# Feed-forward product by tile pairs in seven block products in place of eight, and the output part stepping by pairs on more PSUM banks

## What is computed

```
h = x + LN( Attn( LN(x) ) )          # Wq, Wk, Wv, Wo: 1024x1024, 16 heads of 64, rotary, causal softmax
y = h + LN( FFN( LN(h) ) )           # LN without scale or shift, eps 1e-5
FFN(z) = z @ weight.T + bias + (z @ A.T) @ B.T     # weight 1024x1024; A, B: LoRA factors of rank 16
```

## Time and profile before

| | |
|---|---|
| median of 3 runs | 2083.32 us (2083.1 to 2083.62) |
| profiled execution: its time, its span | 2083.8 us, 2082.0 us |
| PE busy | 1981.3 us (95%), 12192 matmuls |
| DVE, ACT, POOL busy | 1425.8, 866.2, 393.2 us |
| chain of waits that ended last | PE 89%, DVE 4%, DMA 1% |
| costliest line | L603 (the products of the output part): 3072 matmuls |
| granted TensorE clock, mean | 0.979 of full |

### The profile page before, as it was taken

The page is one execution under the profiler, slowest core; times in us unless marked ns, Lnnn a source line. Parts: engine busy times, 40 slices in busy tenths (PEclk is TensorE's granted clock), DMA queues, the critical chain, the costliest instruction groups (busy, mean ns, idle before and its releaser), DMA issues.

```text
span 2082.0 us, 34087 instructions
## 1 busy us (share of the span) xinstructions
PE 1981.3 (95%) x12192; PEld 966.1 (46%) x12192; DVE 1425.8 (68%) x3455; ACT 866.2 (42%) x1985; POOL 393.2 (19%) x393
## 2 busy tenths in 40 slices
PE   4789999999999999999999997699999999999997
PEld 2344444444444444444444443354444444444443
DVE  5787787787787787687787778664554555555554
ACT  6655565565465565465565565421111111111111
POOL 0122222222222222222222222100000000000000
PEclk8999999999999999999999999799999999999998
DMA  8065376465375465375465575924334233433322
GB/s 309 5 128 112 78 143 109 83 142 102 76 145 106 84 141 102 75 144 108 83 141 102 121 205 127 270 74 122 92 76 113 77 102 74 119 102 72 81 61 61
DMA packets 492004, 232.40 MB, mean 112 GB/s; under 512 B 462801, under 2 KB 462929, under 8 KB 490802
## 3 DMA queue, kind: packets, MB, share of 16 engines
q1 hardware_dynamic: 491826, 230.10, 48.1%
HBM read 81.16 MB, written 33.55 MB: 55 GB/s over the span
## 4 chain that ended last, share of the span: by engine, by line
PE 89%; DVE 4%; issue 2%; POOL 1%; ACT 1%; DMA 1%; POOLq 0%; DVEq 0%; ACTq 0%; SPq 0%
PE ps L603 30%; PE ps L486 10%; PE ps L488 10%; PE ps L487 10%; PE ps L511 6%; PE ps L525 5%; PE ps L497 5%; PE ps L499 5%; PE ps L498 5%; PE ps L628 1%; DMA arena<-arena 1%; PE ps L638 1%; PE ps L637 1%; DVE region L692 1%; POOL turn L1182 0%
## 5 line engine op out<-in xcount | busy, mean ns | idle before, releaser
L486 PE MATMUL ps<-arena,region 128*128 128x512 f16 x1024 | 391.1, 382 | 11.0 <-DVE region L692 10.9
L487 PE MATMUL ps<-arena,region 128*128 128x512 f16 x1024 | 390.1, 381 | 0.0
L488 PE MATMUL ps<-arena,region 128*128 128x512 f16 x1024 | 390.1, 381 | 0.0
L877 DVE CUSTOM_DVE_ANT_0 ps<-ps,con,pow 128x384 f32<-128x384 f32 (+3 forms) x512 | 247.0, 555 | 146.9 <-PE ps L511 146.7
L603 PE MATMUL ps<-region,arena 128*128 128x512 f16 x1536 | 338.3, 380 | 0.0
L603 PE MATMUL ps<-region 128*128 128x512 f16 x1536 | 336.9, 379 | 0.2 <-issue 0.2
L1180 POOL TENSOR_TENSOR turn<-turn,con 128x512 f32<-128x512 f32 x128 | 144.3, 1127 | 894.4 <-DVE turn L734 877.2
L1102 ACT ACTIVATE ps<-ps,neg_max 128x384 f32<-128x384 f32 (+3 forms) x512 | 258.2, 510 | 91.9 <-DVE neg_max L877 91.9
L1141 ACT ACTIVATE arena<-ps,sm 128x1024 f32<-128x1024 f32 x64 | 77.1, 1205 | 472.9 <-DVE sm L952 472.9
L747 DVE SCALAR_TENSOR_TENSOR arena<-ps,row_inv,arena 128x384 f16<-128x384 f32 (+3 forms) x512 | 239.6, 542 | 1.0 <-ACT arena L1043 1.0
L1043 ACT ACTIVATE arena<-ps,row_inv 128x384 f16<-128x384 f32 (+3 forms) x512 | 221.2, 543 | 45.4 <-DVE row_inv L760 45.4
(11 more groups left out here) (120 smaller groups left out, 2235.6 us busy)
## 6 DMA issues: line engine op xcount, KB each, us to landing
arena<-x SPq DMA_DIRECT2D x32, 512.0 KB, 3.8
attn_scratch<-o_st SPq DMA_DIRECT2D x64, 256.0 KB, 2.4
region<-attn_scratch SPq DMA_DIRECT2D x8, 2048.0 KB, 8.7
turn<-x SPq DMA_DIRECT2D x32, 512.0 KB, 4.2
out<-v_split SPq DMA_DIRECT2D x32, 512.0 KB, 5.1
arena<-wo SPq DMA_DIRECT2D x8, 1024.0 KB, 7.0
arena<-wf SPq DMA_DIRECT2D x8, 1024.0 KB, 8.2
arena<-wv SPq DMA_DIRECT2D x4, 1024.0 KB, 11.8
```

Source lines behind the costliest of these rows:

```text
L486: mm(o, w[:, k, 0, cols], xnt[par][:, k, 0, :], start=(k == 0), stop=False)
L487: mm(o, w[:, k, 0, cols], xnt[par][:, k, 1, :], start=False, stop=False)
L488: last = mm(o, w[:, k, 1, cols], xnt[par][:, k, 0, :], start=False, stop=(k == KT - 1))
L877: v.tensor_tensor_reduce(out=unit_ps(j, a), in0=unit_ps(j, a), in1=causal[:, 512 - width:512], scale=pow2[:, S_NEG:S_NEG + 1], scalar=HIGH ...
```

## The change

The output part steps by pairs of tiles (`over_pairs`, 16 pairs, 18 steps). The feed-forward product of a pair is a 2x2 block product: the rows are tile 0 and tile 1, the inner dimension and the columns are in two halves of 512. Seven block products (each 4 k-blocks x 3 = 12 matmuls) take the place of eight, with sums of blocks as factors.

- **Weight**: seven fp16 pairs (W11, W22, T1, W21, T3, T2, T4) are made from W_F by `wf_prepare` on DVE (7 low parts and 4 sums for each half of the k-blocks, each 128x1024) and `wf_high_parts` on ACT. Half of this is at the end of the last attention slot, half in step 0.
- **Left side**: besides the four blocks of `xn2`, three sums S2, S4 and S3/S1 are made by four POOL operations (`mix`, 128x512). ACT and DVE split seven blocks where there were four, in operations of 1024, 1536, 512 and 512 columns. SP transposes 28 blocks in one DMA for the high parts, 8 and 20 for the low parts.
- **Products**: `block_product` into banks 4, 5 and 6, with copies of partial results to `y_out` by ACT (m5, m1, m6) and adds by DVE (c12, c22, c11).
- **Wo product**: tile 0 of a pair in banks 0 and 1, tile 1 in banks 2 and 3, both before the feed-forward product of the pair before.
- **`x` tiles**: four buffers. Those of pairs 0 and 1 are loaded in step 0. From step 2 on, SP issues the two loads for pair j in step j, behind the transposes and the stores.
- `lora_split` and `clear_lora` also make the differences `a_diff` and `b_diff`. W_F is loaded in another order.

```diff
@@ sync
+            def step(j, kind, bq, loads):
+                if 1 <= kind <= TP:
+                    need(sp, ff_done, j - 1)
+                    need(sp, x2_high, 4 * j)
+                    sp.nop(nofuse=True)
+                    sp.dma_start_transpose(xt[0][:, :, :], xh).then_inc(xt_h_in, 16)
+                    need(sp, x2_low_a, j)
+                    sp.nop(nofuse=True)
+                    sp.dma_start_transpose(xt[1][:, 0:8, :], xl_a).then_inc(xt_la_in, 16)
+                    need(sp, x2_low_s, 3 * j)
+                    sp.nop(nofuse=True)
+                    sp.dma_start_transpose(xt[1][:, 8:28, :], xl_s).then_inc(xt_ls_in, 16)
...
                 if kind >= 2:
+                    for t in range(2):
+                        slot_x = (2 * kind + t) % 4
+                        sp.wait_ge(y_done, 2 * j - 3 + t)
+                        sp.dma_start(out_tiles[2 * j - 4 + t], y_out[:, t]).then_inc(y_stored[t], 16)
+                        if kind < TP:
+                            sp.dma_start(x2[slot_x], x_tiles[2 * j + t]).then_inc(x_tile_in[slot_x], 16)
+                if kind % 2 == 1 and kind < TP - 4:
+                    sp.wait_ge(ao_done, 2 * j + 2)
+                    load_o(bq + 2, (kind // 2) % 2)
@@ tensor
+            def block_product(xb, wb, bank, start, ks=range(4)):
+                for k in ks:
+                    for hl, wl in ((0, 0), (0, 1), (1, 0)):
+                        last = mm(ps[:, bank, :], xt[hl][:, 4 * xb + k, :], wf[wb][:, k, wl, :],
...
             def step(j, kind, bq, loads):
+                if kind < TP:
...
+                    for a in range(2):
+                        need(pe, u1_done, 2 * j - 1 + a)
+                        if kind == 0 and a == 1:
+                            pe.wait_ge(p_done[1], 8 * PAIRS * B)
+                        ao_product(par, 2 * (kind % 2) + a, BANK_AO[a], kind == 0)
...
+                if 1 <= kind <= TP:
+                    need(pe, xt_h_in, 16 * j)
+                    need(pe, xt_la_in, 16 * j)
+                    need(pe, xt_ls_in, 16 * j)
+                    if kind == 1:
+                        pe.wait_ge(lora_ready, 2)
+                        pe.wait_ge(o_low, PAIRS * B)
+                        pe.wait_ge(wf_low, 14)
+                    need(pe, lt_scaled, j - 1)
+                    lora_first(0, ((A11, a_both, 0), (A12, a_both, 4)))
+                    lora_first(1, ((S1, a_both, 0), (A22, a_diff, 0))).then_inc(lt_done, 1)
+                    need(pe, c12_done, j - 1)
+                    block_product(S1, T1, BANK_53, True).then_inc(m5_done, 1)
+                    need(pe, u2_done[1], 2 * j - 2)
+                    block_product(A11, W11, BANK_U, True).then_inc(m1_done, 1)
+                    need(pe, m5_copied, j)
+                    block_product(S4, W22, BANK_53, False)
+                    need(pe, m1_copied, j)
+                    block_product(S2, T2, BANK_U, False).then_inc(m6_done, 1)
+                    need(pe, lt_low, j)
+                    lora_product(0, BANK_53, b_split[:, :, HALF:D]).then_inc(c12_ready, 1)
+                    need(pe, c11_done, j - 1)
+                    block_product(A12, W21, BANK_2, True, range(2))
+                    need(pe, m6_copied, j)
+                    block_product(S3, T3, BANK_U, False)
+                    lora_product(1, BANK_U, b_split[:, :, HALF:D]).then_inc(c22_ready, 1)
+                    block_product(A12, W21, BANK_2, False, range(2, 4))
+                    lora_product(0, BANK_2, b_split[:, :, 0:HALF]).then_inc(c11_ready, 1)
+                    need(pe, c22_done, j)
+                    block_product(A22, T4, BANK_U, False)
+                    lora_product(1, BANK_U, b_diff).then_inc(ff_done, 1)
@@ vector: order of one step
+            def step(j, kind, bq, loads):
+                if kind >= 2:
+                    need(dve, ff_done, j - 1)
+                    stats([c21, c22], st2[1], mv2[1], bn2_done, mv2_done, 2 * j - 3)
...
+                    s_low(j, 0, xl_s[:, 0:1536], xn2_f[:, 1024:2560], xh[:, 1024:2560])
...
+                    s_low(j, 1, xl_s[:, 1536:2048], xs2_f, xh[:, 2560:3072])
+                    s_low(j, 2, xl_s[:, 2048:2560], xs4_f, xh[:, 3072:3584])
...
+                        v.tensor_tensor(y_out[:, a], x2[(2 * kind + a) % 4], y_out[:, a], ALU.add).then_inc(y_done, 1)
+                if kind < TP:
+                    for a in range(2):
+                        residual(j, kind, bq, a)       # the residual chain; waits for x_tile_in before the add
+                if kind == 0:
+                    o_evac(PAIRS * B - 1, 1)
+                    wf_prepare(1, 0)
...
+                    v.tensor_scalar(t_part, ps[LOW_ROW:LOW_ROW + LR, BANK_T, 0:256], adapter[:, tile],
...
+                    v.tensor_tensor(t_stack[LOW_ROW:LOW_ROW + LR, :], t_f, t_stack[0:LR, :],
                                     ALU.subtract).then_inc(lt_low, 1)
+                if kind < TP:
+                    need(dve, x2_high, 4 * j + 1)
+                    need(dve, xt_la_in, 16 * j)
+                    v.tensor_tensor(xl_a, xn2[0], xh[:, 0:1024], ALU.subtract).then_inc(x2_low_a, 1)
+                if 1 <= kind <= TP:
...
+                    v.tensor_tensor(c12, ps[:, BANK_53, :], c12, ALU.add).then_inc(c12_done, 1)
...
+                    v.tensor_tensor(c22, ps[:, BANK_U, :], c22, ALU.add).then_inc(c22_done, 1)
...
+                    v.tensor_tensor(c11, ps[:, BANK_2, :], c11, ALU.add).then_inc(c11_done, 1)
...
+                    stats([c11, c12], st2[0], mv2[0], bn2_done, mv2_done, 2 * j - 2)
@@ scalar: order of one step
+                    normalise(y_out[:, 0], y_out[:, 0], sm2[0], u2_done[0])
...
+                    x_high(xh[:, 1024:2560], xn2_f[:, 1024:2560])
...
+                    x_high(xh[:, 2560:3072], xs2_f)
...
+                    x_high(xh[:, 3072:3584], xs4_f)
...
+                        normalise(xn2[a].rearrange("p (c n) -> p c n", c=2), ps[:, BANK_AO[a]:BANK_AO[a] + 2, :], sm1,
+                                  u1_done)
...
+                    x_high(xh[:, 0:1024], xn2[0])
...
+                    s.activation(y_out[:, 1, HALF:D], ps[:, BANK_53, :], ACT.Copy).then_inc(m5_copied, 1)
...
+                    s.activation(y_out[:, 0, 0:HALF], ps[:, BANK_U, :], ACT.Copy).then_inc(m1_copied, 1)
...
+                    s.activation(y_out[:, 0, HALF:D], ps[:, BANK_U, :], ACT.Copy).then_inc(m6_copied, 1)
@@ gpsimd
+                    need(pool, xn2_done, 2 * j + 2)
...
+                    mix(xn2_f[:, 2048:2560], xn2_f[:, 1024:1536], xn2_f[:, 1536:2048], ALU.add)
+                    need(pool, x2_mix, 4 * j + 1)
+                    mix(xn2_f[:, 1024:1536], xn2_f[:, 0:512], xn2_f[:, 1024:1536], ALU.subtract)
+                    mix(xs2_f, xn2_f[:, 2048:2560], xn2_f[:, 0:512], ALU.subtract)
+                    need(pool, x2_mix, 4 * j + 3)
+                    mix(xs4_f, xn2_f[:, 512:1024], xs2_f, ALU.subtract)
```

More of the change, by code:

```diff
@@ L173, in sandwich_kernel @@
         a_raw = arena1[:, 5120:5120 + KT * LR].rearrange("p (k r) -> p k r", k=KT)
         a_both = half(arena1[:, 5504:5504 + KT * 64], ("p (k r) -> p k r", dict(k=KT)))
[L175 to L182, removed]
+        a_diff = half(arena1[:, 6400:6656], ("p (k r) -> p k r", dict(k=4)))
@@ new lines, in sandwich_kernel @@
+        t_part = arena1[0:LR, 5120:5376]
+        t_f = arena1[0:LR, 6016:6272]
+        t_stack = arena1[:, 6272:6400].bitcast(F16)
+        xn2_f = arena1[:, 6656:9216]
+        xn2 = [xn2_f[:, 1024 * a:1024 * a + 1024] for a in range(2)]
+        xs2_f, xs4_f = arena1[:, 3584:4096], arena2[:, 3584:4096]
+        xh = v_f[:, 2048:3840].bitcast(F16)
+        xl_a = xn_low_t[:, :]
+        xl_s = con[:, C_MASK:C_MASK + 1280].bitcast(F16)
+        xt = [half(arena1[:, 1792 * n:1792 * n + 1792], ("p (k t) -> p k t", dict(k=28))) for n in range(2)]
@@ L259, in sandwich_kernel @@
         rm2_done = sem("rm2_done")
-        u2_done = sem("u2_done")
+        u2_done = [sem(f"u2_done{a}") for a in range(2)]
         y_done = sem("y_done")
@@ new lines, in ao_product, with lora_product @@
+                last.then_inc(ao_done, 1)
+            def block_product(xb, wb, bank, start, ks=range(4)):
+                for k in ks:
+                    for hl, wl in ((0, 0), (0, 1), (1, 0)):
+                        last = mm(ps[:, bank, :], xt[hl][:, 4 * xb + k, :], wf[wb][:, k, wl, :],
+                                  start=(start and k == 0 and hl == 0 and wl == 0),
+                                  stop=(k == 3 and hl == 1), skip_group_check=True)
+                return last
+            def lora_product(t, bank, factor):
+                for hl in range(2):
+                    last = mm(ps[:, bank, :], t_stack[:, 128 * t:128 * t + 128], factor[:, hl, :],
+                              start=False, stop=(hl == 1), skip_group_check=True)
+                return last
@@ L620, in step @@
                     pv_products(PAIRS - 1)
```

(16 more changed lines are left out.)

397 lines of the change are left out of this document (242 added, 155 removed).

## The result

The changed kernel takes 2143.27 us (median of 4 runs, 2140.06 to 2149.16) against 2083.21 for the kernel before (median of 4). The ratio is 1.0294, with a 95% interval from 1.0274 to 1.0313. The forecast was 2128, with a range from 2098 to 2150. The profiled execution took 2143.08 us, with a span of 2141.3.

A forecast was written before the change was run, and what follows sets the result against it. PE was taken as the bound before the change. Start to 1433.3, 14 steady steps of 46.1, then 16.0 + 23.9 + 9.1 gave 2127.7 us of span; likeliest median 2128, range 2098 to 2150.

The forecast's parts named there:

- step that carried the forecast: Steady step: tile 0's add waits for the late load of x, landing at 19.5; the step takes load + 26.6 us.
- m5 gaps: Steady step, before the third block product: PE waits 2.7 us for ACT's m5 copy, ready at 30.4, wanted at 27.7.
- "worse" rival: POOL's third sum also wins (2145), or the clock falls in each step's 2.7 us gap (2160); chance 0.16.
- second gap: Steady step, before the first `lora_product`: PE waits for DVE's `t_stack`, ready at 36.5 against 35.6.
- band of 2121 to 2135: The forecast's own case: steady steps of 45.6 to 46.6 us; chance 0.50.
- the cast: LoRA operation on DVE after `xn2`: by the rule it waits and ends with POOL's first sum; no row showed it.
- the third sum: Steady step: if POOL's third sum also comes before the last LoRA operation, the step takes 47.3 us, 2145 in all.
- a choice between 46.1 and 45.1: Steady step in us: 46.1 if the LoRA cast waits for POOL by the rule, 45.1 without it.
- The rule on transposes: SP's three transposes: 7.0 us at the skill's 261 GB/s, in place of 8.6 at the rows' 213; chance 0.05.
- The last gap: End, pair 15, no Wo product above it: PE idles 16.0 us for the transposes before the last feed-forward product.
- The floor: Steady steps with PE always busy: 42.36 us per pair, after 2.6 us less work; span would be 2075.
- "Faster": Steady steps: PE stays the bound, x arrives in time, load landed by 16.3; 2076 us, chance 0.10.

The follow-up runs named there:

- e5_three: Changed kernel with x loads ahead of the last transpose, m5 copy before normalising tile 1, LoRA operations inside tile 1's chain: 2077.01 us, ratio 0.9954.

## Why the prediction was right

**The load of `x`.** The step that carried the forecast held, and both experiments on it show it: with the load earlier, 65 of the 68 us lost in the steady steps are back, and with the add 0.4 us later each step takes 0.4 us more. In the step from 1759.22 the order of events was met item by item: transposes from 5.0 (5.1 predicted), the load out at 14.7 (14.5), landing at 20.0 in that step (19.5), m5 copy 10.3 after the add starts (10.9 by the prediction's own times).

**The size.** The prediction had 2127.7 us of span, and 2141.3 came. The steady steps took 661.2 us in place of 645.4, 15.8 more; the start took 2.2 less, and the end was met. Two terms were too small. I had the load out at 14.5 and took its landing at 5.0 from rows 3, bounds 4.2 to 6.5; in the mean of the 14 steps it went out at 14.85 and the add began 5.6 later, at 20.5 and not 19.5. DVE's wait for it came out at 92.3 / 14 = 6.6 us a step where 19.5 meant 5.6, and the m5 gaps are 3.0 in the mean, not 2.7. Why a load takes longer to land here than in the kernel before, no run separates. And the clock, which I had only in the "worse" rival: in nine of the 14 steps matmuls at a lower clock behind the m5 gap cost 18.6 us in all, 1.3 a step. The second gap was smaller than the 0.9 in the sum: it shows in the five steps at full clock and in none of the nine others, since PE at the lower clock reaches that point later.

So the mechanism was right, and the number only in part. The measured time lies above the band of 2121 to 2135 that had 0.50, in the part of the range that was there for the worse rival (0.16), and that rival's condition on the clock came true in nine steps. That the time still lies within 16 us of the forecast is partly luck: the sum had 0.9 a step for the second gap, 12.6 us in all, and it came to 3.7, which made up for a part of the missing clock. In the same way the step is the start of the add plus 26.7 us in the mean (47.2 - 20.5), where the forecast had 26.6, by terms that offset each other. Adding up the last line of the sum again gives 2083.3 + 45.7 = 2129, not 2128.

**POOL and DVE.** The sum let the cast wait for POOL's first sum, and the last LoRA operation for the second. The trace has 0.42 and 1.44 us where the operations alone take 0.28 and 0.42, so both waited; L1142 ended at 1795.66, 2.88 after POOL began, where two sums and the operation are 2.96. It did not wait for the third sum: between two POOL operations without a wait, DVE came in. That rival is settled. The 0.15 us held against L662's 0.54 is the time of one-column operations; L662 itself runs once, beside POOL, so those rows could not settle the cast. Rows and rule (the Trainium skill, SBUF — State Buffer, Who interferes with whom) had left a choice between 46.1 and 45.1; the trace agrees with the rule: 0.42 us beside POOL, and 0.28 in all 16 pairs when POOL waits.

**The rule on transposes.** The Trainium skill's 261 GB/s (DMA: Bandwidth & Descriptors, Latency and other measured facts) isn't reached by these, if the time that an issue holds SP is taken for the transfer's. The issue of 28 blocks took 4.27 us, which is 215 GB/s, as the rows of before had it.

**Start and end.** The first feed-forward product started at 1407.8 (1409.4 predicted), behind a gap of 23.0 (25.1), and the steady part began at 1431.1 (1433.3). The last gap was 15.7 (16.0). `lora_split` and `clear_lora` shifted the first Wo product by 3.4 us, from 1336.43 to 1339.87 (3.3 predicted).

**The floor.** 42.36 us per pair was reached in e5_three. The sum for it, 2075 us of span, comes within 1.5 us of the 2076.5 of that run.

**The rivals.** "Faster" was given 0.10 and needed the load to land by 16.3. That was the right condition: with the load moved, the adds of tile 0 begin at 15.1 to 16.4 us, and the kernel is faster. In the kernel as changed they begin at 19.6 to 22.1.

## What to carry to other kernels

When a loop step is widened, look at which DMAs are issued in the same step as their use, and at what now stands ahead of them in the issuing queue: a load that went out 9 us ahead of its use can slide behind work that has just grown 3.5 times (56 blocks to transpose in a step, where there were 16), and here that cost 68 us in the steady steps, where the arithmetic saved 36. The engine that the bottleneck waits for is where a delay surfaces; follow that engine's own queue back to an operation that waits for a DMA, and undo that before reordering anything else. Price start and end apart from the steady steps: in a two-stage pipeline of 16 steps they took 35 of 41 us.

## What the runs showed of the hardware

A gap of PE of two to three microseconds can cost nearly as much again through the clock, and not each time. The length of the gap alone doesn't decide it. In the changed kernel the clock stayed at full behind 2.09, 2.11, 2.27, 2.71 and 2.98 us of idle time, and fell behind 2.20, 2.56, 2.65 and the six gaps of 3.25 to 4.63. The matmuls behind it then took 1.6 to 2.9 us more. Behind 2.11 us it was at 1.00 (1743.6), behind 2.56 at 0.59 in the mean of the row below (1789.6), behind 3.92 at half (1647.7). Windows of the changed kernel, where the third column from the right is the granted clock:

```profile
1743.60:1747.00 3.40, 3.37 (x16) 1.58 (x17) 2.57 (x6) 0.46 (x1) 0.77 (x2) 1.00 0.00 0
...
1789.60:1793.00 3.40, 3.37 (x10) 1.27 (x11) 2.57 (x6) 0.46 (x1) 0.77 (x2) 0.59 0.00 0
```

```profile
1647.70:1651.00 3.30, 3.27 (x8) 1.19 (x9) 2.47 (x6) 0.46 (x1) 0.68 (x2) 0.50 0.00 0
```

The run where POOL waits has two gaps of almost one length, behind the same 24 matmuls: 2.21 us (to 1460.49), then 0.68 in the mean of the first row, and 2.22 us (to 1555.34), then full clock.

```profile
1460.50:1463.90 3.40, 3.40 (x11) 1.32 (x12) 2.57 (x6) 0.42 (x1) 0.55 (x1) 0.68 0.00 0
1555.40:1558.80 3.40, 3.40 (x16) 1.51 (x17) 2.57 (x6) 0.37 (x1) 0.55 (x1) 1.00 0.00 0
```

POOL and DVE take turns when both have two-input work in SBUF. In the start of the changed kernel, POOL's four sums took 7.89 us where four of 1.27 are 5.1, and DVE's operations of 1.2 between them took 1.9 to 2.3:

```profile
1377.41 7.89 POOL L1412 TENSOR_TENSOR arena<-arena 128x512 f32<-128x512 f32 x4 [0.93 <-DVE arena L1101]
1377.85 1.91 DVE L969 SCALAR_TENSOR_TENSOR region<-arena,pow,region 128x1024 f16<-128x1024 f32 x1
...
1379.80 2.17 DVE L973 TENSOR_TENSOR arena<-arena 128x1024 f32<-128x1024 f32 x1
```
